# A six-block decoder on one core: delta rule reordered at its start and end, cross-attention results turned in 32x32 squares on VectorE, maxima turned once for two groups of heads

## The reference

```
x = x + delta_rule(layernorm(x))              # 8 heads of 128; conv of 4 taps, S = S*alpha + k (v - k S) beta
x = x + cross_attention(ctx, layernorm(x))    # 16 heads of 16 channels, masked, softmax over 375
x = x + experts(layernorm(x))                 # best 2 of 8
x = x + causal_attention(layernorm(x))
x = x + cross_attention_2(layernorm(x), ctx)  # the same with biases on q, k, v
x = x + ffn(layernorm(x))
```

## Time and profile before

| | us |
|---|---|
| before, median of 3 runs (1881.64 to 1888.5) | 1884.56 |
| the profiled execution: its time | 1882.25 |
| its span in the trace | 1880.6 |

### The profile page before, as it was taken

How to read it: one execution, slowest core, us unless ns; L and a number is a source line. 1 busy time by engine, 2 the same in 40 slices (tenths; PEclk the granted TensorE clock), 3 DMA queues, 4 the chain that set the end, 5 groups by cost and what they waited for, 6 DMA issues and landing times.

```text
span 1880.6 us, 39028 instructions
## 1 busy us (share of the span) xinstructions
PE 1794.2 (95%) x14700; PEld 1291.1 (69%) x14700; DVE 1187.6 (63%) x3215; ACT 694.4 (37%) x1816; POOL 654.1 (35%) x694
## 2 busy tenths in 40 slices
PE   5679999999999999999999999999999999999999
PEld 2457777777766666665445666666659979889698
DVE  4668888888657777777766667777765234243332
ACT  3224444444344555553001456555632222122221
POOL 1344442443215667665000266666624000000000
PEclk9879999999999999999999999999999999999999
DMA  6212122221113111110000001010040000000000
GB/s 196 47 36 47 30 42 42 41 39 22 22 33 120 48 33 48 34 34 21 1 1 1 11 22 33 22 28 26 12 180 1 6 6 1 10 1 1 10 1 10
DMA packets 106953, 61.94 MB, mean 33 GB/s; under 512 B 79944, under 2 KB 102800, under 8 KB 106000
## 3 DMA queue, kind: packets, MB, share of 16 engines
q1 hardware_dynamic: 106624, 59.39, 12.0%
q10 hardware_dynamic: 144, 0.06, 0.0%
HBM read 53.91 MB, written 5.51 MB: 32 GB/s over the span
## 4 chain that ended last, share of the span: by engine, by line
PE 79%; DVE 6%; issue 5%; POOL 5%; ACT 2%; DMA 2%; SPq 1%; DVEq 0%; POOLq 0%; ACTq 0%
PE ps L2540 18%; PE ps L1554 6%; PE ps L605 5%; PE ps L1576 5%; PE ps L2412 5%; PE ps L2072 5%; PE ps L1593 4%; PE ps L1625 4%; PE ps L2618 3%; PE ps L725 2%; PE ps L1610 2%; POOL w L577 2%; PE ps L1691 2%; PE ps L1563 2%; DVE big_b L949 2%
## 5 line engine op out<-in xcount | busy, mean ns | idle before, releaser
L1985 POOL TENSOR_TENSOR h_w<-h_w 125x336 int32<-125x336 int32 x384 | 335.3, 902 | 202.9 <-ACT h_w L1784 202.9
L1870 DVE CUSTOM_DVE_ANT_0 h_w<-ps,h_w 112x375 f32<-112x375 f32 x512 | 262.3, 541 | 0.1
L949 DVE SCALAR_TENSOR_TENSOR big_b<-ps,taps,big_b 128x444 f32<-128x444 f32 (+2 forms) x288 | 193.9, 673 | 70.0 <-ACT big_b L827 56.3
L1784 ACT ACTIVATE h_w<-ps 125x336 f32<-125x336 f32 x512 | 196.5, 464 | 21.6 <-PE ps L1576 21.6
L277 POOL TENSOR_TENSOR rstd<-var_eps,minus_half 112x4 f32<-112x4 f32 x12 | 12.2, 1017 | 407.9 <-DVE var_eps L264 407.9
L1576 PEld LDWEIGHTS ps<-h_w 32*125 32x125 f32 x3072 | 97.2, 183 | 68.5 <-issue 67.7
L1576 PE MATMUL ps<-h_w 32*125 32x112 f32 x3072 | 118.0, 282 | 12.6 <-DVE h_w L1870 7.2
L605 PE MATMUL ps<-h_w,kq_w 128*128 128x448 f32 x256 | 115.7, 577 | 14.9 <-DVE h_w L969 14.9
L1554 PE MATMUL ps<-h_w 32*112 32x375 f32 x1024 | 120.5, 519 | 0.9 <-DVE h_w L1870 0.9
L2072 PE MATMUL ps<-expert_w,big_a 128*112 128x512 f32 x256 | 114.1, 597 | 0.0
L1879 DVE TENSOR_TENSOR h_w<-h_w,ps 128x112 f32<-128x112 f32 x128 | 34.7, 271 | 120.0 <-PE ps L1563 120.0
(11 more groups left out here) (363 smaller groups left out, 3667.8 us busy)
## 6 DMA issues: line engine op xcount, KB each, us to landing
h_w<-in_h SPq DMA_DIRECT2D x2, 4096.0 KB, 16.8
kq_w<-in_ctxT SPq DMA_DIRECT2D x16, 375.0 KB, 3.7
h_w<-in_ctxT SPq DMA_DIRECT2D x16, 375.0 KB, 3.8
big_a<-decays SPq DMA_DIRECT2D x16, 196.0 KB, 3.0
w<-decays SPq DMA_DIRECT2D x16, 196.0 KB, 3.0
h_w<-in_mask SPq DMA_DIRECT2D x16, 164.1 KB
h_w<-in_maskT SPq DMA_DIRECT2D x16, 164.1 KB
kq_w<-in_kq_w SPq DMA_DIRECT2D x8, 256.0 KB, 3.8
```

Source lines behind the costliest of these rows:

```text
L949: dve.scalar_tensor_tensor(p3(dst)[:, :, i:], p3(ps[:, bank, 0:GT])[:, :, 0:T - i], k.taps[:, h, n, TAPS - 1 - i:TAPS - i], p3(dst)[:, :, ...
L1784: act.activation(k.PTx[(4 * Q + r) % RING][0:CK], ps[0:CK, turned_bank(Q, r), 0:NC * T], ACT.Exp).then_inc(s["exp"], 1)
L1870: dve.tensor_tensor_reduce(k.masked[r % 2], ps[0:T, score_bank(Q, r), 0:S2], k.mask_add[n % 2], -1.0, 3.0e38, ALU.add, ALU.min, k.neg_max[ ...
L1985: pool.tensor_tensor(P.bitcast(I32), P.bitcast(I32), k.mask_W[n % 2], ALU.mult).then_inc(s["weights"], 1)
```

## The change

**Start.** The gates are projected token-major at once (gdn_xT as the stationary operand, 16 columns moving) into one bank, so the ScalarE copies and the turns go; VectorE reads all 16 sequences with two instructions; the gate chain is put ahead of the convolutions of unit 0 on ScalarE and VectorE. 16 products of the identity are put ahead of the first turn on TensorE. On SP `cumulative(6)` goes ahead of `exchange(0)` and `cumulative(7)` into it, ahead of its 8 last DMAs; GpSimd's first join of head 0 comes one unit later.

**Last units.** `exchange(7)` is taken one unit earlier on SP, and VectorE finishes the rows of head 7 in the unit where it begins them, ahead of `tail(u - 1, 5)`.

**Cross-attention.** `turned`, exponentials and masks handle quad s-2 instead of s-1, `apply` quad s-3. `maxima` runs at every second step (q 0 and 2), for quads s-2 and s-1 together, and VectorE then does both `less_maximum`. The last third of the values leaves `early` of q 2 and becomes `values_2`, `late` of the same step; its evacuation moves to the front of ScalarE's q 3. `output_turn`, `output_back`, and `oa` go: VectorE turns the sums from PSUM in 32x32 squares (`tokens`, 128x512, q 3, after maximum 1; `apply` of the next sequence waits for it), divides (`normalize`, now 128 partitions), and turns back (`channels`, 128x256, next q 0, after maximum 1). In layer 0 this gives `onT`; in layer 1 it gives `on_raw`, and ScalarE adds the bias at q 0 after three exponentials. The output product stays at q 0, `late`.

The diff, cut to its core:

```diff
-    for c in range(KD):
-        ins = pe.matmul(k.ps[0:16, gate_bank(g), 0:GT], k.ba_w[:, c, :], k.gdn_xT[:, g, c, :], start=(c == 0), stop=(c == KD - 1))
+    for j in range(G):
+        at = (G * g + j) * 2 * HEADS
+        for c in range(KD):
+            ins = pe.matmul(k.ps[0:T, GATE_BANK, at:at + 2 * HEADS], k.gdn_xT[:, g, c, j * T:(j + 1) * T], k.ba_w[:, c, :],
+                            start=(c == 0), stop=(c == KD - 1))
...
+    for _ in range(16):
+        pe.matmul(ps[:, 7, 0:128], k.ident[:, :], k.ident[:, :], start=True, stop=True)
...
     act.wait_ge(s["c_gdn"], 96)
+    start_act_soft_plus(act, k, s)
     keys(0, 0)
-    start_act_soft_plus(act, k, s)
...
     dve.wait_ge(s["c_gdn"], 96)
+    start_dve_gate_in(dve, k, s)
+    start_dve_gate_out(dve, k, s)
     keys(0, 2)
-    start_dve_gate_in(dve, k, s)
     keys(0, 3)
-    start_dve_gate_out(dve, k, s)
...
-        if a == NG + 1:
+        if a == NG + 2:
             join(pool, k, s, 0, 0)
...
+        if between is not None:
+            cumulative(between)
         sp.wait_ge(s["zeros"], 2)
...
-            if is_unit(unit + 2):
+            if is_unit(unit + 2) and unit not in (NG, NG + 1):
                 cumulative(unit + 2)
...
-        h = head_due(u, 3) if u >= 0 else 0 if unit == NG - 1 else None
+        if unit == NG - 1:
+            cumulative(NG + 2)
+            exchange(0, NG + 3)
+        h = (head_due(u, 4) if is_late(u) else head_due(u, 3)) if u >= 0 else None
...
         if h4 is not None:
-            rows(h4, range(4, 7))
+            rows(h4, range(4, HALF + 2))
+            rows_first(dve, k, s, h4)
         if h2 is not None:
             join(dve, k, s, h2, 3)
         tail(u - 1, 5)
+        if h3 is not None:
+            join(dve, k, s, h3, 1)
...
 def turned_bank(Q, r):
-    return (8 * Q + 12 + r) % POOL_BANKS
+    return r if Q == QUADS * B - 1 else (8 * Q + 2 + r) % POOL_BANKS
...
-        pe.wait_ge(s["qx"], Q + 1)
+        pe.wait_ge(s["qx"], Q + 1 if Q % 2 else Q + 2)
         if Q:
             pe.wait_ge(s["exp"], 4 * Q)
-        if Q < last:
-            pe.wait_ge(s["max"], 4 * Q + 6)
+        if Q < last - 1:
+            pe.wait_ge(s["max"], 4 * Q + 10)
...
+    def values_2(seq):
+
+        n = base + seq
+        pe.wait_ge(s["ctx_sum"], n + 1)
+        pe.wait_ge(s["qz"], n + 1)
+        values(n, 2, KD * T).then_inc(s["v2_proj"], 1)
...
-        elif q == 2 and is_sequence(seq - 1):
-            output_turn(seq - 1)
-        elif q == 3 and is_sequence(seq - 1):
-            if is_sequence(seq + 1):
-                pe.wait_ge(s["k_sb"], 4 * n + 6)
-            output_back(seq - 1)
+        elif q == 2 and is_sequence(seq + 1):
+            values_2(seq + 1)
...
-        before, b_q = quad_at(step - 1)
-        ago, a_q = quad_at(step - 2)
+        before, b_q = quad_at(step - 2)
+        ago, a_q = quad_at(step - 3)
...
-        if is_sequence(before):
+        if is_sequence(before) and b_q % 2 == 0:
             maxima(before, b_q)
...
+        elif l and q == 0 and is_sequence(seq - 2):
+            act.wait_ge(s["on_raw"], seq - 1)
+            act.wait_ge(s["o_proj"], n - 2)
+            for c in range(KD):
+                ins = act.activation(k.onT[:, c * 128:c * 128 + T], k.on_raw[:, c * 128:c * 128 + T], ACT.Identity, bias=k.xb_col[:, 2, c:c + 1])
+            ins.then_inc(s["onT"], 1)
...
-        dve.tensor_tensor(k.Qx[Q % 2], k.Qz[n % 2][:, z, m, :], ps[:, turned_bank(Q, 0), NC * T:(NC + 1) * T], ALU.add).then_inc(s["qx"], 1)
+        dve.scalar_tensor_tensor(k.Qx[Q % 2], ps[:, turned_bank(Q - z, 0), NC * T:(NC + 1) * T], k.k_keep[:, 2 + z:3 + z],
+                                 k.Qz[n % 2][:, z, m, :], ALU.mult, ALU.add).then_inc(s["qx"], 1)
...
+        dve.wait_ge(s["PV"], 4 * (n + 1))
+        dve.transpose(k.o_tok, squares(ps[:, 6, :], QUADS)).then_inc(s["o_tok"], 1)
...
+            dve.transpose(squares(k.onT, KD), k.on).then_inc(s["onT"], 1)
+        else:
+            if seq:
+                dve.wait_ge(s["onT"], n)
+            dve.transpose(squares(k.on_raw, KD), k.on).then_inc(s["on_raw"], 1)
...
+        if is_sequence(before) and b_q % 2 == 0:
             less_maximum(before, b_q)
+            less_maximum(before, b_q + 1)
         if is_sequence(seq):
             maximum(seq, q, 0)
             maximum(seq, q, 1)
+        if q == 3 and is_sequence(seq - 1):
+            tokens(seq - 1)
+        if q == 0 and is_sequence(seq - 2):
+            channels(seq - 2)
```

More of the change, by code:

```diff
@@ L34 @@
 EVEN = 1.0e-30
+SQUARE = 32
 W_FIRST = 16 * 11
@@ L357, in start_dve_gate_in @@
     dve.wait_ge(s["c_ba"], 48)
[L358 to L364, removed]
+    dve.wait_ge(s["ba"], NG)
+    ba = k.ps[0:T, GATE_BANK, 0:2 * ALL].rearrange("p (s c) -> p s c", s=B)
+    dve.tensor_tensor(y, ba[:, :, HEADS:], k.dt_bias[:, :].unsqueeze(1).to_broadcast([T, B, HEADS]), ALU.add)
+    dve.tensor_copy(bb, ba[:, :, 0:HEADS]).then_inc(s["ba_in"], 1)
 def start_dve_gate_out(dve, k, s):
@@ L1095, in gdn_dve @@
             rows(h4, range(1, 4))
[L1096 to L1100, removed]
         solve(u, "less")
@@ L1227, in gather, with exchange @@
             sp.dma_start(square(half(k.C_full, e)), pairs(k.nd[h % 2, :, :, FIRST, SECOND])).then_inc(s["c_in"], 16)
-    def exchange(h):
+    def exchange(h, between=None):
         sp.wait_ge(s["tri"], SMALL_DONE * (h + 1))
@@ L1804, in middle @@
             cross_norm_act(act, k, s, l, seq + 1, 7)
-        elif q == 3:
-            if is_sequence(seq - 1):
-                act.wait_ge(s["onT_ps"], n)
-                if n >= 2:
-                    act.wait_ge(s["o_proj"], n - 1)
-                if l == 0:
-                    ins = act.activation(k.onT, ps[:, 7, 0:KD * T], ACT.Copy)
-                else:
-                    for c in range(KD):
-                        ins = act.activation(k.onT[:, c * T:(c + 1) * T], ps[:, 7, c * T:(c + 1) * T], ACT.Identity,
-                                             bias=k.xb_col[:, 2, c:c + 1])
-                ins.then_inc(s["onT"], 1)
+        elif l and q == 0 and is_sequence(seq - 2):
[4 more added lines that the diff above has]
+            ins.then_inc(s["onT"], 1)
     for step in range((B + 1) * QUADS + 1):
         seq, q = quad_at(step)
-        before, b_q = quad_at(step - 1)
+        before, b_q = quad_at(step - 2)
         n = base + seq
@@ L1850, in cross_act @@
             weights(before, b_q, 3)
-        if l == 0 and (seq, q) == (B, 0):
+        if l == 0 and (seq, q) == (B, 1):
             gating_act(act, k, s, 0, 9)
+        elif l and (seq, q) == (B, 3):
+            ffn_act_gate(act, k, s, 0, 1)
 def cross_dve(dve, k, s, l):
@@ L1909, in cross_dve @@
         seq, q = quad_at(step)
-        before, b_q = quad_at(step - 1)
-        ago, a_q = quad_at(step - 2)
+        before, b_q = quad_at(step - 2)
+        ago, a_q = quad_at(step - 3)
         if q == 1 and is_sequence(seq - 2) and seq < B:
             add_output(seq - 2)
-        if q == 3 and is_sequence(seq - 1):
-            normalize(seq - 1)
-        if is_sequence(before):
+        if step == 0 and l == 0:
+            dve.wait_ge(s["On"], UNITS)
+            dve.wait_ge(s["gdn_x"], UNITS)
+            dve.memset(ps[:, 6, :].rearrange("p (q t) -> p q t", q=QUADS)[:, :, T:], 1.0).then_inc(s["setup_dve"], 1)
+        if is_sequence(before) and b_q % 2 == 0:
             less_maximum(before, b_q)
+            less_maximum(before, b_q + 1)
         if is_sequence(seq):
@@ L1926, in cross_dve @@
             maximum(seq, q, 2)
+        if q == 3 and is_sequence(seq - 1):
+            normalize(seq - 1)
         if q == 0 and seq and is_sequence(seq + 1):
```

184 lines of the change are left out of this document (70 added, 114 removed).

## The result

| | us | ratio to before (95% interval) |
|---|---|---|
| before, median | 1883.38 | |
| the changed kernel, median (1916.75 to 1925.15) | 1921.68 | 1.0202 (1.0178 to 1.0226) |
| its profiled execution: time, span | 1916.75, 1915.4 | |

The forecast was 1884 (range 1864 to 1902), with faster, same and slower at about a third each. The time is 38 above before and 20 above the range's end.

A forecast was written before the change was run, and what follows sets the result against it. TensorE was taken as full except for waits early and a few later stops. From the profiled 1882.25, start -16.7, last units -4.6, layer 0 +5.7, layer 1 +14, fill and drain +2 gave 1882.7, placed at 1884 us (1864 to 1902).

The forecast's parts named there:

- Gates: Start: softplus at 24.6, 8.4 earlier; first N0 from 51.61 to about 43.5, 8 us gained, bounds 6 and 9.
- Exchange of head 0: Start: cumulative(7) moved ahead brings N0 of unit 7 from 117.4 to 108.7, 8.7 us gained.
- Last units: TensorE's stop shrinks by 1.3 and splits; the clock holds, 3.3 more: 4.6 us gained, at worst 0.5.
- rival D: Last units: the stop stays above 2 us and the clock falls; 4 more, 1888; chance counted within the forecast's 0.48.
- Cross-attention, layer 0: Four steps sum to 19.73 us a sequence against 19.34, +0.39, in all +5.7 us.
- The floor from scores to turned: Cross-attention, q 2 and q 0: VectorE's chain keeps turned scores from starting sooner than 2.8 us after scores.
- the bias wait: Layer 1, q 0: the output product waits for bias copies behind three exponentials, 5.4 against 4.37; layer 1 term +14 us.
- Fill and drain: Cross-attention's ends: a pipeline one step deeper costs +2 us in all, 0 to 5.
- The square turn: Cross-attention, q 3: VectorE's 128x512 turn from PSUM takes 0.68 us, 1.36 if at half rate.
- rival B: Cross-attention, q 3: the square turn is slow, 1.36 us, adding 21 us: 1905; chance 0.14.
- Rival A: Cross-attention's floors are softer, bias copies or second less_maximum partly hidden: 1862 to 1870; chance 0.24.
- Rival C: Start: a DMA or the join still holds N0 of unit 7, only the gates' 8 come through: 1893; chance 0.14.

The follow-up runs named there:

- e14: The kernel of e1 with 12 more identity products between the first and second turn: 1864.96 us, ratio 0.9906.
- e13: The kernel of e1 without the 16 identity products ahead of the first turn: 1872.12 us, ratio 0.9943.
- e1: The kernel before with only the changes to the start and the last units, cross-attention as before: 1869.29 us, ratio 0.9933.
- e12: The kernel of e1 without the changes to the gates: 1873.80 us, ratio 0.9960.
- e11: The kernel of e1 without the changes to the last units: 1870.82 us, ratio 0.9947.
- e8: The kernel of e4 with GpSimd masking 16 of 336 columns, result not valid: layer 0 sequence 19.90 us, from 20.46; total time not read.
- e5: The changed kernel with the transpose of maxima of q 0 and q 2 between the second and third score: 1950.41 us.
- e2: The changed kernel with ScalarE's two layer 1 bias copies ahead of the exponentials of their step: 1902.43 us.
- e9: The changed kernel with the bias copies ahead of the exponentials and the last third of the values back behind the queries: 1878.09 us, ratio 0.9974.
- e4: The changed kernel with the reciprocal and multiplication of q 3 behind maximum 3 on VectorE: 1929.02 us.

## Why the prediction was wrong, point by point

**Gates: the step that failed is the price of the lower clock.** I put the last turn at 20, the last two projections at 24 and softplus at 24.6, and allowed 2 us for projections at the lower clock (the lower bound of 6). In the changed kernel everything from some 16 us to past 29 ran at that level, the turns included. The last two groups, 32 of the 64 matmuls that the trace has for the gates, started at 23.14 and took 6.02; softplus began at 29.89 and the first N0 came at 47.45, not 43.5: 4.2 gained, below the lower bound. With the level held (e14) the same two groups took 3.23 from 19.93 on, softplus began at 23.89, and the first N0 came at 41.44, 10.2 gained and above the upper bound of 9. So the projections were priced about rightly for the upper level. The 16 added products, which I had at nothing, gave 1.85 at the first N0 (e13 against e1).

**Exchange of head 0: right.** From the end of the inversion to N0 of unit 7 I summed 26.9 and measured 27.8 (77.80 to 105.60); e12, without the gates, gained 7.9 of the 8.7. The wait moved from the place where the earlier trace rows show it to the join and the three parts behind it, as followed.

**Last units: mechanism named, size wrong.** The start gave 11.8 at unit 7, and from there to the first score another 1.3 was gained; e11 against e1 puts 1.5 (within the noise) on the last units, not 4.6. The stop in front of the turn of results did shrink, to 0.45 (it is 3.99 in e11, without these hunks), and the new wait for the tail is 0.89 (0.8 forecast). But the joined blocks, which come back through DRAM, were next (argued from the order, since the view names no releaser). The clock fell behind the new stop as it had behind the one in the earlier trace rows; it was granted at 0.57 from 500 to 504, and the output product took 3.15 and not 1.98:

```profile
498.09 0.99 PE L649 MATMUL ps<-expert_w,h_w 112*112 112x84 f32 x8 [2.08 <-issue]
499.00 0.41 PE L675 MATMUL ps<-h_w 84*28 84x28 f32 x8
499.34 3.15 PE L705 MATMUL ps<-gdn_out_w,big_b 128*112 128x256 f32 x8
```

VectorE ended its last part at 492.2 and wrote; 5.9 later the product of L649 started. My text followed what is late next as far as the tail, and not to the read behind the join. This was rival D, and its price of 4 was about right (4.6 less 1.3 is 3.3).

**Cross-attention, layer 0: +0.39 a sequence forecast, +0.91 measured.** (0.39 times 15 is 5.9; the 5.7 in the sum is a slip that changes nothing.) The floor from scores to turned (2.8) and q 2 stood. The step that failed is the pair q 3 and q 0. I let VectorE's list of q 3 end at 4.4 and wrote that the next second score waits for it, and then priced q 0 as if its scores took 0.83. The wait had to be carried on: 4.62 to the last maximum of q 3, then a second pass of scores, then transpose, two `less_maximum`, two maxima. 10.12 for both steps against 9.82. e8 shows the carry, e5 the second pass. The rest (0.13 at q 2, 0.09 at q 1) is small and of one sign.

**Layer 1: the bias wait was right** (5.4 less 4.37 is 1.03 forecast, 1.01 idle and 1.08 a step measured, e2), with layer 0's 0.5 on top.

**Fill and drain: +2 forecast, 13.6 measured.** I priced one more round by the work that it adds; in the drain TensorE's idle time grew by 3.7 in layer 0, and the granted clock went down as well. It is the largest term that was mis-sized. That depth is what costs is argued; the size is measured, in e9 too.

**The square turn: right.** 0.71 measured, 0.68 taken; rival B is out.

```profile
L1849 DVE STREAM_TRANSPOSE big_b<-ps 128x512 f32<-128x512 f32 x14 | 10.0, 711 | 0.0
L1866 DVE STREAM_TRANSPOSE big_b<-big_b 128x256 f32<-128x256 f32 x14 | 6.2, 441 | 0.0
```

The Trainium skill ("Vector Engine (DVE) Microarchitecture Reference", 3.8) gives one element per cycle and lane. The slope agrees, 0.27 for 256 elements more, if PSUM and SBUF inputs cost the same; the estimate of 0.53 worked out from it left out a fixed part, 0.17 by these two rows.

**Rival A** pointed the wrong way: the floors were as hard as worked out. **Rival C** was near the start's truth (some of the 16.7 is lost) for another reason. No rival had the carry or the drain, so the range had no room on the side where both lay.

## What to carry to other kernels

In a pipeline of steps whose engines take turns, write the wait that crosses a step's end into the next step's first term before taking floors; a sum of per-step floors is too low when one engine ends late. Price the extra depth of a pipeline at its ends, where each wait stands bare and the clock can fall, once for each time it drains (7.5 and 6.2 here, with the cause argued). Instructions removed from a full engine are a gain only down to the next wait that their time kept hidden: e9 has them all removed and gains 0.08 a sequence in layer 0, nothing in layer 1.

## What the runs showed of the hardware that I had not expected

- Two VectorE instructions that work in SBUF alone took most of a GpSimd instruction's rest on top when they started just behind it: the 128x256 multiplication 0.97 to 1.12 in place of 0.43, the 125x336 mask up to 1.02 in place of 0.33 (e4 and the changed kernel, against e8). In one sequence of the changed kernel a start 0.36 later became 1.05 in all.
- Scores in four row tiles run side by side: two take 0.82, four 0.83 (e5). What parted them, a transpose (e5) or a late maximum (q 0), cost up to a whole pass.
- 12 products of no use (24 matmuls in the trace, 2.9 us) made the whole kernel 4 us faster (e14 against e1). Without them a gap of 1.7 us (2.2 in the changed kernel) ahead of busy work was followed by the lower clock (0.50) until past 29 us.
- In e13 the granted clock reads 1.00 in the same stretch, while a matmul of the gates takes 0.19 as at 0.50 in the changed kernel. The kernel before reads 1.00 too, while its first two turns take 1.73 and 1.75 and the third 0.99. So at the beginning of these kernels the durations tell the level, not that column, and what I wrote ahead of e13 of the kernel before was read from the column. The window of e13 (busy times, then 1.00 as the granted clock):

```profile
25.00:29.00 4.00, 4.00 (x23) 4.00 (x23) 0.00 (x0) 0.00 (x0) 0.00 (x0) 1.00 0.72 250
```
